# Two turns reordered: the last stage's step 0 begun in chunk 13, and the expert sums moved behind the scan

## The chip, the cores and the metric

The kernel runs on one core of a Trainium2 chip. The metric is the device time of one execution in microseconds (us), the median of a few runs. TensorE (PE) multiplies into eight PSUM banks, VectorE (DVE), ScalarE (ACT) and GpSimd (POOL) work elementwise, SyncE (SP) issues most DMAs; each runs its own queue of instructions in order and waits on semaphores for the others.

## The reference

A block on x of shape (8, 256, 32, 32): a layer norm over channels, a selective scan over 1024 tokens in a permuted order, a residual, then a mixture of experts on tokens.

```python
xz = silu(einsum('oc,bchw->bohw', in_proj_w, ln_c(x)) + in_proj_b)      # 256 -> 768
x_ssm, res, gate = split(xz, 3, axis=1)
xf = silu(conv1d_depthwise(x_ssm, dw_w, 3 taps) + dw_b)
dbc = einsum('oc,bcn->bon', dbc_w, xf) + dbc_b                          # dt, B, C per head
# two heads; x, softplus(dt), B, C gathered by perm (argsort of a Moebius score)
h = exp(dt * A) * h + dt * B * x;  y = sum_s(h * C) + D * x             # S = 8, 1024 steps
x = x + silu(out_proj(gather(y, inv) * silu(gate) + res) + out_b)
t = tokens(x);  u = ln_t(t)
w = softmax(u @ gate_w + gate_b); w = w * (w >= 0.1); w = w / sum(w)
out = t + sum_e w[:, e] * (u @ expert_w[e] + expert_b[e])               # 8 experts, 256 -> 256
```

## The kernel before

Float32 is multiplied as a high and a low part in fp32r (split3: three products). There are three stages, written out engine by engine, with an order set by hand.

Stage 1 takes the eight images ("batches", b = 0 to 7): norm, input projection (in_proj, L1211, weights win), convolution, and for each token a row of x, dt, B and C, stored to HBM (store_rows, L450) and later gathered by rank (gather_rows, L713). The residual and gate parts go to HBM from rg (L492, L501). Batch 7 is woven with the begin of stage 2. In it TensorE also runs expert_sums (L1298 to L1306), sums over the channels of the expert and gate weights, which are needed only in stage 3, and VectorE copies them in bias_rows. Batch 6's rows are stored by ScalarE here (L949).

Stage 2 is the scan, in 16 chunks q of 64 tokens for two heads of four images. For each: sums of dt (sums_of), B and C turned to rows (rows_of, L1268) and split to high and low (ScalarE rows_high L927, VectorE rows_low L1907) in the tile r6, which SP stores to bc_scratch (L457) and loads back spread over partitions (spread: eight loads L464 into cr, one L466 into bl); sums of dt between pairs of tokens (times_of, L1277) and from these dists (L1897); columns (L1317), which waits for r6 of the chunk after; eight products of B and C (products, L1332) in three banks, which VectorE multiplies by ScalarE's exponentials (decays L1012, times_decay L1947 and L1950); GpSimd adds six of these (add_state, L750); VectorE joins the sum to the tile kbd (whole_kernel, L1962); the chunk after runs y (y_states L1383, y_kernel L1391), which ScalarE copies out (y_rows L1026) and SP stores. cr and rg, the latter as ee, take over memory of stage 1, so parts of cr are set to zero behind the last in_proj (zero_rows L1816, and ScalarE L1047 for half of cr1). GpSimd issues the gathers of the rows three chunks ahead, and in chunks 9 to 12 (gather_first, L761) those of y for the first half image of stage 3.

Stage 3 takes 16 half images v (two for an image). For each: y gathered into token order and transposed (L1446), times gate (first_gate L2186, gate_y L2023), plus residual on GpSimd (first_z L773, z_of L825), high and low (z_high L1067, low_z L2029), out_proj (L1473) into banks FRONT_BANKS = (5, 4) for step 0, silu (L1077), residual x (L2046), transposes to tokens (L1485), statistics (L2053) and rstd on GpSimd (L829), gate logits (L1495, L1504), softmax (softmax_in, gate_exp L1097, softmax_out), whose weights TensorE transposes (weights_by_experts), and 16 products of experts (L1531). One step's front is woven into the experts of the step before; step 0's front is woven into chunks 14 and 15 (first_y_by_channels, first_gate and first_z in body(q), the rest in last_body and last_chunks). The z of all steps is split into zh and zl, in the first half columns of xhl, which is also cr[0].

## Time and profile before

| | us |
|---|---|
| median of 3 runs | 957.85 (956.61 to 958.96) |
| profiled execution | 963.8 |
| its span, first to last instruction | 962.1 |
| PE busy | 881.6 (92%) |
| DVE busy | 738.8 (77%) |
| ACT busy | 515.9 (54%) |
| POOL busy | 483.9 (50%) |

Times in the rows are us from the start of the span. Stage 1 ends near 244, stage 2 runs to about 461 and overlaps with stage 3's step 0. Busy shares are means over stages of unlike kind, so the page alone doesn't tell what bounds a turn. A row in order of time gives start, duration, line, tiles, and in brackets the idle time of the engine before it, with what ended it.

### The profile page before, as it was taken

What the parts mean: (1) busy time and instruction counts of PE and PEld (TensorE: products, weight loads), DVE (VectorE), ACT (ScalarE), POOL (GpSimd) and SP (SyncE); (2) the same over time, 40 slices, a digit from 0 to 9 for tenths busy, and PEclk for the clock granted to TensorE, in tenths of its full rate; (3) what the DMA queues carried; (4) which work ended last, traced back from release to release, by engine and by line L of the source; (5) the groups of instructions that cost most, each with busy time, mean ns of one, the idle gap of its engine ahead of it and who ended that gap; (6) DMA issues with size and microseconds to landing.
All of it is one profiled execution on the core that took longest, in us unless ns stands there. A gap on an engine that the chain in (4) does not pass through costs nothing.

```text
span 962.1 us, 15548 instructions
## 1 busy us (share of the span) xinstructions
PE 881.6 (92%) x4568; PEld 684.7 (71%) x4568; DVE 738.8 (77%) x2010; ACT 515.9 (54%) x1011; POOL 483.9 (50%) x552
## 2 busy tenths in 40 slices
PE   5999999899588788777999999999999999999997
PEld 4888888787355455545777777778777877777776
DVE  5769888564588888876878788787878877878875
ACT  4788777765799999885332333333233323323320
POOL 2165578885678787878363424244144442341100
PEclk8999999999688988979999999999999999999999
DMA  6235775466445544543530402304114132040000
GB/s 179 104 119 179 203 204 183 140 132 166 126 118 163 175 143 149 176 118 121 202 100 23 175 30 77 133 22 157 40 44 153 38 131 71 22 174 22 22 20 25
DMA packets 63689, 110.07 MB, mean 114 GB/s; under 512 B 18538, under 2 KB 44436, under 8 KB 60564
## 3 DMA queue, kind: packets, MB, share of 16 engines
q1 hardware_dynamic: 54388, 90.23, 29.6%
q0 software_dynamic: 7168, 18.03, 6.6%
q10 hardware_dynamic: 2080, 1.19, 0.8%
q8 instruction: 23, 0.38, 0.2%
q14 instruction: 30, 0.25, 0.1%
HBM read 61.51 MB, written 47.92 MB: 114 GB/s over the span
## 4 chain that ended last, share of the span: by engine, by line
PE 61%; DVE 13%; POOL 9%; DMA 6%; ACT 5%; issue 5%; SPq 1%; another core or an unknown queue 0%; DVEq 0%; POOLq 0%; ACTq 0%
PE bank L1531 33%; POOL sm L750 6%; PE bank L1211 6%; PE bank L1473 5%; PE bank L1446 3%; PE bank L1495 2%; DVE ssm L2023 2%; PE bank L1332 2%; PE bank L1391 2%; DMA score_scratch<-score 1%; PE bank L1383 1%; PE bank L1222 1%; PE bank L1485 1%; ACT dtri L1020 1%; PE bank L1520 1%
## 5 line engine op out<-in xcount | busy, mean ns | idle before, releaser
L813 POOL DMA_INDIRECT xtm<-y_scratch,idxu x112 | 116.2, 1037 | 75.7 <-DVE idxu L2015 44.8
L1531 PE MATMUL bank<-wexph,xhl 128*128 128x512 f32 x512 | 143.3, 401 | 1.3 <-DVE xhl L2068 1.3
L1531 PE MATMUL bank<-wexph,cr 128*128 128x512 f32 x512 | 142.4, 400 | 0.0
L825 POOL TENSOR_TENSOR ssm<-ssm,rg 128x512 f32<-128x512 f32 x30 | 35.2, 1195 | 149.1 <-DVE ssm L2023 149.1
L1531 PEld LDWEIGHTS bank<-wexph,xhl 128*128 128x128 f32 x512 | 93.3, 188 | 22.7 <-issue 2.1
L1531 PEld LDWEIGHTS bank<-wexph,cr 128*128 128x128 f32 x512 | 93.5, 188 | 20.2
L750 POOL TENSOR_TENSOR sm<-sm,rg 128x512 f32<-128x512 f32 x80 | 102.7, 1284 | 6.1
L1012 ACT ACTIVATE rg<-dists,aown 128x512 f32<-128x512 f32 x128 | 82.0, 723 | 5.7 <-POOL sm L750 5.7
L1947 DVE TENSOR_TENSOR rg<-rg,bank 128x512 f32<-128x512 f32 x112 | 72.3, 680 | 15.6 <-PE bank L1332 13.8
L1531 PE MATMUL bank<-wexpl,xhl 128*128 128x512 f32 x256 | 80.7, 396 | 0.0
L1531 PE MATMUL bank<-wexpl,cr 128*128 128x512 f32 x256 | 80.4, 395 | 0.0
L1072 ACT ACTIVATE ssm<-bank,outb 128x512 f32<-128x512 f32 x30 | 20.6, 688 | 85.3 <-PE bank L1473 52.8
L2139 DVE SCALAR_TENSOR_TENSOR xf<-bank,soft,xf 128x256 f32<-128x256 f32 x128 | 57.1, 478 | 10.0 <-remote 8.4
L2139 DVE SCALAR_TENSOR_TENSOR ysb<-bank,soft,ysb 128x256 f32<-128x256 f32 x128 | 57.1, 478 | 7.3 <-PE bank L1531 5.2
L877 ACT ACTIVATE rg<-bank,inb 128x512 f32<-128x512 f32 x64 | 43.4, 687 | 35.2 <-PE bank L1211 33.6
L1211 PE MATMUL bank<-xhl,winh 128*128 128x512 f32 x192 | 57.2, 421 | 3.9 <-ACT ssm L877 2.9
L1147 ACT ACTIVATE stage<-bank 128x512 f32<-128x512 f32 x32 | 17.5, 596 | 73.9 <-PE bank L1446 70.5
L1211 PE MATMUL bank<-cr,winh 128*128 128x512 f32 x192 | 55.6, 412 | 1.3 <-ACT rg L877 0.6
L1531 PEld LDWEIGHTS bank<-wexpl,xhl 128*128 128x128 f32 x256 | 48.3, 189 | 11.6
L1531 PEld LDWEIGHTS bank<-wexpl,cr 128*128 128x128 f32 x256 | 48.2, 188 | 11.3
L829 POOL TENSOR_TENSOR rstd<-mv,root 128x4 f32<-128x4 f32 x16 | 16.6, 1041 | 77.3 <-DVE mv L2059 77.2
L2144 DVE SCALAR_TENSOR_TENSOR ysb<-bank,soft,ysb 128x256 f32<-128x256 f32 x128 | 55.5, 475 | 0.0
(329 smaller groups left out, 2077.7 us busy)
## 6 DMA issues: line engine op xcount, KB each, us to landing
xin<-in_x SPq DMA_DIRECT2D x16, 1024.0 KB, 6.9
res_gate_scratch<-rg SPq DMA_DIRECT2D x16, 1024.0 KB
rg<-res_gate_scratch SPq DMA_DIRECT2D x8, 2048.0 KB
y_scratch<-ysb SPq DMA_DIRECT2D x16, 512.0 KB, 2.9
out<-stage SPq DMA_DIRECT2D x16, 512.0 KB, 2.7
rows_scratch<-stage SPq DMA_DIRECT2D x8, 580.0 KB
bc_scratch<-r SPq DMA_DIRECT2D x16, 288.0 KB
rows_scratch<-xr SPq DMA_DIRECT2D x6, 580.0 KB
```

The source lines that it names most:

```text
L750: pool.tensor_tensor(ksum[c.two], ee[:, 0, :] if s == 1 else ksum[c.two], ee[:, s, :], ALU.add).then_inc(summed.sem, 1)
L813: pool.indirect_dma_start(out=xtm[:, t, h * P:(h + 1) * P], out_offset=None, in_=y_d[b // GB].rearrange("q p s c -> (q p s) c"), in_offset ...
L825: pool.tensor_tensor(z[:, k, :], z[:, k, :], rg[:, k, cols], ALU.add).then_inc(z_ready.sem, 1)
L877: act.activation(dst, bank[2 + hf][:, :], ACT.Silu, bias=inb[:, m:m + 1]).then_inc(mm_used[hf].sem, 1)
L1012: act.activation(ee[:, s, :], dist[c.two].rearrange("p t n -> p (t n)"), ACT.Exp, scale=aown[:, s:s + 1]).then_inc(e_ready.sem, 1)
L1211: last = pe.matmul(bank[2 + hf][:, :], w[:, k, m * P:(m + 1) * P], v[:, k, cols], start=(n + k == 0), stop=(n + k == 3))
L1446: last = pe.transpose(dst[:, i * P:(i + 1) * P], src(i), ident[:, :])
L1473: last = pe.matmul(bank[banks[m]][:, :], w[:, k, m * P:(m + 1) * P], x_[:, k, :], start=(n + k == 0), stop=(n + k == 3))
L1531: last = pe.matmul(bank[4 + i][:, :], x_[:, k, i * P:(i + 1) * P], w[:, 2 * ep * KC + k:2 * ep * KC + k + KC + 1:KC, :], start=(n + k == 0 ...
L1947: dve.tensor_tensor(ee[:, s, :], ee[:, s, :], bank[BC_BANK + s % 3][:, :], ALU.mult).then_inc(bc_used[s % 3].sem, 1)
L2139: dve.scalar_tensor_tensor(ttm[par][:, i, :], bank[4 + i][:, 0:C], soft[par][:, 1, i, 2 * ep:2 * ep + 1], ttm[par][:, i, :], ALU.mult, ALU ...
L2144: dve.scalar_tensor_tensor(ttm[par][:, i, :], bank[4 + i][:, C:2 * C], soft[par][:, 1, i, 2 * ep + 1:2 * ep + 2], ttm[par][:, i, :], ALU.m ...
```

## The change

It has two parts. At the first turn: expert_sums leaves batch 7 and is cut in three parts (12, 10 and 10 matmuls, now into bank 0), set between TensorE's work after chunk 15's products; bias_rows follows statistics3; batch 6's rows are stored by SP, at the head of its batch 7, instead of by ScalarE; chunk 1's rows_of, rows_high and rows_low come before chunk 0's first product; the upper part of cr1 is set to zero by GpSimd in one memset of 128x3072 behind the gathers of chunks 2 and 3, instead of by VectorE (128x1024) and ScalarE (128x2048).

At the second turn: first_y_by_channels, first_gate and first_z move from chunk 14 to chunk 13; z_high and low_z follow in chunk 14, and zh and zl lie now in win's tiles; out_proj's halves come before chunk 15's products 1 and 4; on GpSimd three gathers leave the midst of chunk 15's additions and stand behind them with the two that were there; ScalarE takes chunk 15's columns, and an exponential of one column, earlier. All work of the kernel before is still done. The diff, cut to one line of context:

```diff
@@ -201,7 +201,8 @@
 gate_sums = sb("gate_sums", [P, E])
-ones = hs[1][:, :]
+cw1 = sb("all_ones", [P, P])
+ones = cw1[:, :]
...
@@ -225,7 +226,7 @@
        for v in (xf[:, 0, :], ysb[0][:, :, :].rearrange("p s n -> p (s n)"))]
-zh, zl = (xhl[:, v, :, 0:HALF] for v in range(2))
+zh, zl = (w[:, :, :].rearrange("p k c -> p (k c)")[:, 0:KC * HALF].rearrange("p (k n) -> p k n", n=HALF) for w in win)
...
@@ -457,7 +458,7 @@
 if c.q == 1:
-    sync.wait_ge(cr_zero[1], 5)
+    sync.wait_ge(cr_zero[1], 4)
...
@@ -487,6 +488,8 @@
     load_experts(b)
+if b == NB - 1:
+    store_rows(b - 1)
...
@@ -732,10 +735,14 @@
 up_to_token(Chunk(1))
-softplus_ratio(softplus_power(NB - 1))
...
 gather_rows(Chunk(3))
+last_front = softplus_power(NB - 1)
+for hf in range(2):
+    pool.wait_ge(mm_full[hf].sem, mm_full[hf].at(NB, 0))
+pool.memset(cr1[:, 2:S, :].bitcast(F32), 0.0).then_inc(cr_zero[1], 1)
+softplus_ratio(last_front)
...
@@ -775,10 +782,8 @@
 for s in range(1, S - 1):
-    if q == CHUNKS - 2 and s in (S - 3, S - 2):
+    if q == CHUNKS - 3 and s in (S - 3, S - 2):
         first_z(s - S + 3)
-    if q == CHUNKS - 1 and s == 3:
-        gather_first(1, second_half[3:6])
...
@@ -800,7 +805,7 @@
 if q == CHUNKS - 1:
-    gather_first(1, second_half[6:8])
+    gather_first(1, second_half[3:8])
...
@@ -912,13 +917,13 @@
     act.wait_ge(h_ready.sem, h_ready.at(c.q - 1, 0))
-if c.q == 0:
-    act.wait_ge(rows_split.sem, rows_split.at(0, 1))
+if c.q < 2:
+    act.wait_ge(rows_split.sem, rows_split.at(c.q, 1))
...
-if c.q:
+if c.q > 1:
...
@@ -940,14 +945,6 @@
                 act.activation(cwt[c.four][:, :], bank[A_BANK][:, 0:P], ACT.Copy).then_inc(cols_copied.sem, 1)
-
-            def store_rows(b):
-
-                act.wait_ge(rows_ready.sem, rows_ready.at(b, 4))
-                act.wait_ge(rows_staged.sem, rows_staged.at(b, 4))
-                for hf, v in enumerate(staged[b % 2]):
-                    act.dma_start(rows_d[b // GB][:, hf * TPH * HEADS:(hf + 1) * TPH * HEADS, b % GB, :],
-                                  v.rearrange("p t (h c) -> p (t h) c", h=HEADS)).then_inc(rows_stored[b % 2].sem, 16)
...
@@ -976,7 +973,6 @@
 block_decays(Chunk(0))
-store_rows(b - 1)
...
@@ -1038,14 +1034,11 @@
 c = Chunk(q)
-rows_high(Chunk(q + 1))
+if q:
+    rows_high(Chunk(q + 1))
+else:
+    state_decay(Chunk(1))
 block_decays(Chunk(q + 1))
-if q == 0:
-    act.wait_ge(kbd_zero, 1)
-    for hf in range(2):
-        act.wait_ge(mm_full[hf].sem, mm_full[hf].at(NB, 0))
-    act.activation(cr[1][:, S // 2:S, :], bc(kbd[:, 0:GB, :].rearrange("p t n -> p (t n)"), 1, S // 2),
-                   ACT.Copy).then_inc(cr_zero[1], 1)
...
@@ -1096,6 +1089,7 @@
+rows_high(Chunk(1))
...
@@ -1106,24 +1100,25 @@
 columns(c)
+z_high(0)
...
     y_rows(Chunk(CHUNKS - 3), h)
-z_high(0)
+columns(last)
 decays(last, 2, S)
-columns(last)
 first_silu_t(0)
-states_by_tile(last)
...
 x3_high(0, 0)
+states_by_tile(last)
...
 y_rows(c, 1)
+act.activation(std[:, 0:1], root[:, 0:1], ACT.Exp)
...
 y_rows(last, 0)
+gate_exp(0, 0)
 y_rows(last, 1)
-gate_exp(0, 0)
...
@@ -1274,6 +1269,8 @@
 pe.wait_ge(dist_set.sem, dist_set.at(c.q, 0))
+if c.q == CHUNKS - 1:
+    pe.wait_ge(y_gated.sem, y_gated.at(0, KC))
...
@@ -1291,20 +1288,21 @@
-            def expert_sums():
-
-                pe.wait_ge(kbd_zero, 6)
-                pe.wait_ge(wexp_low, WEXP_PARTS)
-                pe.matmul(bank[1][0:2 * E, 0:C], ident[0:E, 0:2 * E], expb[:, :], start=True, stop=False)
-                for e in range(E):
+            def expert_sums(lo, hi):
+
+                pairs = [(e, k, w) for e in range(E) for k in range(KC) for w in wexp]
+                if lo == 0:
+                    pe.wait_ge(kbd_zero, 6)
+                    pe.wait_ge(wexp_low, WEXP_PARTS)
+                    pe.wait_ge(h_ready.sem, h_ready.at(CHUNKS, 0))
+                    pe.matmul(bank[0][0:2 * E, 0:C], ident[0:E, 0:2 * E], expb[:, :], start=True, stop=False)
+                for e, k, w in pairs[lo:hi]:
+                    last = pe.matmul(bank[0][0:2 * E, 0:C], minus_one[:, E - 1 - e:3 * E - 1 - e], w[:, e * KC + k, :],
+                                     start=False, stop=(e, k) == (E - 1, KC - 1) and w is wexp[1])
+                if hi == len(pairs):
                     for k in range(KC):
-                        for w in wexp:
-                            last = (e, k) == (E - 1, KC - 1) and w is wexp[1]
-                            pe.matmul(bank[1][0:2 * E, 0:C], minus_one[:, E - 1 - e:3 * E - 1 - e], w[:, e * KC + k, :],
-                                      start=False, stop=last)
-                for k in range(KC):
-                    last = pe.matmul(bank[1][:, C:C + E], ones, gateraw[:, k, :], start=(k == 0), stop=(k == KC - 1))
-                last.then_inc(sums_full, 1)
+                        last = pe.matmul(bank[0][:, C:C + E], ones, gateraw[:, k, :], start=(k == 0), stop=(k == KC - 1))
+                    last.then_inc(sums_full, 1)
...
@@ -1323,7 +1321,6 @@
 pe.wait_ge(dskip_ready, 4)
-pe.wait_ge(sums_taken, 4)
...
@@ -1354,7 +1351,6 @@
 sums_of(Chunk(0))
-expert_sums()
...
@@ -1362,8 +1358,8 @@
 sums_of(Chunk(1))
+rows_of(Chunk(1))
 products(Chunk(0), 0, 1)
-rows_of(Chunk(1))
...
@@ -1406,14 +1402,14 @@
 products(c, 1, 4)
-if q == CHUNKS - 2:
+if q == CHUNKS - 3:
...
 products(c, 4, 6)
-if q == CHUNKS - 2:
+if q == CHUNKS - 3:
...
@@ -1431,15 +1427,16 @@
 columns(c)
+out_proj(0, FRONT_BANKS, 0, 1)
+products(c, 1, 4)
+out_proj(0, FRONT_BANKS, 1, 2)
+products(c, 4, 6)
...
     y_states(prior, h)
-products(c, 1, 4)
-out_proj(0, FRONT_BANKS, 0, 1)
-products(c, 4, 6)
-out_proj(0, FRONT_BANKS, 1, 2)
...
     y_kernel(prior, h)
+expert_sums(0, 12)
...
@@ -1449,7 +1446,7 @@
 pe.wait_ge(gathered[0].sem, gathered[0].at(1, 0))
-pe.wait_ge(dist_set.sem, dist_set.at(CHUNKS, 0))
+pe.wait_ge(dist_set.sem, dist_set.at(CHUNKS - 1, 0))
...
@@ -1465,7 +1462,8 @@
 if banks == FRONT_BANKS:
-    pe.wait_ge(cols_copied.sem, cols_copied.at(CHUNKS, 0))
+    pe.wait_ge(*((dist_set.sem, dist_set.at(CHUNKS, 0)) if lo == 0 else
+                 (cols_copied.sem, cols_copied.at(CHUNKS, 0))))
...
@@ -1575,12 +1573,14 @@
 y_states(Chunk(CHUNKS - 1), 0)
+expert_sums(12, 22)
...
 y_states(Chunk(CHUNKS - 1), 1)
+expert_sums(22, 2 * E * KC)
...
@@ -1813,7 +1813,8 @@
     dve.wait_ge(mm_full[hf].sem, mm_full[hf].at(b, 0))
-dve.memset(cr[i][:, 2:S if i == 0 else S // 2, :].bitcast(F32), 0.0).then_inc(cr_zero[i], 1)
+if i == 0:
+    dve.memset(cr[i][:, 2:S, :].bitcast(F32), 0.0).then_inc(cr_zero[i], 1)
...
@@ -1849,7 +1850,6 @@
 exponents(Chunk(0))
-bias_rows()
...
@@ -1965,13 +1965,11 @@
 c = Chunk(q)
-if q + 1 < CHUNKS:
+if 0 < q < CHUNKS - 1:
...
     whole_kernel(Chunk(q - 1))
-if q == CHUNKS - 1:
-    low_z(0)
...
@@ -1980,22 +1978,26 @@
 times_decay(c, 4)
-if q == CHUNKS - 2:
+if q == CHUNKS - 3:
...
 times_decay(c, 5)
-if q == CHUNKS - 2:
+if q == CHUNKS - 3:
...
 if q == CHUNKS - 1:
-    first_residual()
+    first_residual(0)
+    clear_wide(0, Chunk(q - 1))
+    first_residual(1)
...
     next_states(Chunk(q + 1))
+if q == CHUNKS - 2:
+    low_z(0)
...
@@ -2038,13 +2040,17 @@
-            def first_residual():
+            def first_residual(k):
...
                 dve.wait_ge(x3_ready.sem, x3_ready.at(0, 16))
-                for k in range(KC):
-                    dve.wait_ge(m3_free[k].sem, m3_free[k].at(0, 1))
-                    dve.tensor_tensor(tcm[:, k, :], bank[FRONT_BANKS[k]][:, :], xin[:, k, 0:HALF], ALU.add).then_inc(
-                        t_ready.sem, 1)
+                dve.wait_ge(m3_free[k].sem, m3_free[k].at(0, 1))
+                dve.tensor_tensor(tcm[:, k, :], bank[FRONT_BANKS[k]][:, :], xin[:, k, 0:HALF], ALU.add).then_inc(
+                    t_ready.sem, 1)
+
+            def clear_wide(par, c):
+
+                dve.wait_ge(k_ready.sem, k_ready.at(c.q, 2))
+                own.did(dve.memset(wide[par], 0.0))
...
@@ -2207,6 +2213,7 @@
 zero_rows(1, NB)
+rows_low(second)
...
@@ -2220,13 +2227,12 @@
 statistics3(front, 0, 0)
+bias_rows()
 shifts(front, 0)
-dve.wait_ge(k_ready.sem, k_ready.at(CHUNKS, 0))
-for v in wide:
-    own.did(dve.memset(v, 0.0))
-own.settle()
...
 front.end()
+clear_wide(1, Chunk(CHUNKS - 1))
+own.settle()
...
     step3(b, 1, True, b + 1)
```

## Rows read from the trace of the kernel before

**Rows 1.** Stretches: us, busy per engine (count), PEclk, DMA share, GB/s.

```profile
303.00:413.00 110.00, 87.99 (x505) 57.34 (x504) 91.12 (x216) 102.53 (x298) 91.35 (x79) 0.91 0.54 160
...
440.00:466.00 26.00, 21.15 (x102) 15.57 (x103) 18.30 (x47) 13.93 (x28) 16.51 (x15) 0.93 0.46 169
466.00:962.00 496.00, 482.39 (x2336) 380.58 (x2334) 392.48 (x1101) 151.02 (x228) 166.95 (x157) 1.00 0.22 76
```

**Rows 2.** Chain that ended last, chunks 0 to 3: start, us, what.

```profile
219.79 3.85 PE bank L1303 x32
...
238.03 5.80 DMA bl<-bc_scratch
...
243.88 0.80 PE bank L1332
...
322.39 3.06 DMA bl<-bc_scratch
```

**Rows 3.** SP's DMA issues: start, us, line, what.

```profile
207.05 1.00 SPq L450 DMA_DIRECT2D rows_scratch<-stage  x2
208.78 0.71 SPq L501 DMA_DIRECT2D res_gate_scratch<-rg  x1
...
230.82 0.50 SPq L457 DMA_DIRECT2D bc_scratch<-r  x1
234.17 3.82 SPq L464 DMA_DIRECT2D xhl<-bc_scratch  x8
...
268.30 2.72 SPq L464 DMA_DIRECT2D xhl<-bc_scratch  x8
```

**Rows 4.** DMA queue q1, 207 to 215.5: packets, MB, share.

```profile
q1 hardware_dynamic: 2080, 1.19, 96.1%
```

**Rows 5.** DMA queue q1, 228 to 231.9.

```profile
q1 hardware_dynamic: 144, 1.05, 63.8%
```

**Rows 6.** DMA queue q0 (gathers), 245 to 251.

```profile
q0 software_dynamic: 320, 1.19, 70.6%
```

**Rows 7.** POOL in order of time, batch 7 and chunk 0.

```profile
223.60 0.56 POOL L657 TENSOR_TENSOR xr<-dbx,xr 128x64 f32<-128x64 f32 x2
...
243.38 1.10 POOL L713 DMA_INDIRECT xr<-rows_scratch,turn  x1 [0.95 <-DMA rows_scratch<-xr]
...
253.18 1.29 POOL L750 TENSOR_TENSOR sm<-rg 128x512 f32<-128x512 f32 x1 [4.66 <-DVE rg L1947]
```

**Rows 8.** PE in order of time, chunk 0.

```profile
249.06 0.48 PE L1317 MATMUL bank<-ident,cw 128*128 128x128 f32 x1 [2.71 <-DVE r L1909]
```

**Rows 9.** POOL in order of time, chunks 12 to 15.

```profile
416.41 0.95 POOL L761 DMA_INDIRECT ssm<-y_scratch,idxu  x1 [0.30 <-issue]
...
429.28 1.28 POOL L750 TENSOR_TENSOR sm<-rg 128x512 f32<-128x512 f32 x1 [3.85 <-DVE rg L1947]
...
455.45 0.96 POOL L761 DMA_INDIRECT xtm<-y_scratch,idxu  x1
...
458.99 1.05 POOL L829 TENSOR_TENSOR rstd<-mv,root 128x4 f32<-128x4 f32 x1 [1.33 <-DVE mv L2059]
```

**Rows 10.** DMA queue q0 (gathers), 419 to 419.5.

```profile
q0 software_dynamic: 4, 0.00, 2.3%
```

**Rows 11.** PE in order of time, chunks 13 to 15.

```profile
415.44 1.91 PE L1383 MATMUL bank<-xf,cwt 128*128 128x512 f32 x2
...
419.59 1.02 PE L1383 MATMUL bank<-xf,cwt 128*128 128x512 f32 x2
...
433.36 0.66 PE L1446 MATMUL bank<-ident,ssm 128*128 128x128 f32 x4 [1.22 <-DVE ssm L2186]
...
465.52 0.61 PE L1446 MATMUL bank<-ident,sm 128*96 128x128 f32 x4 [0.64 <-DVE sm L2112]
```

**Rows 12.** DVE in order of time, chunk 14.

```profile
439.40 1.40 DVE L1962 TENSOR_TENSOR kbd<-sm,bank 64x512 f32<-64x512 f32 x2 [0.82 <-POOL sm L750]
```

**Rows 13.** ACT in order of time, end of chunk 15.

```profile
461.38 1.28 ACT L1097 ACT_TABLE_LOAD   x1
```

More of the change, by code:

```diff
@@ L1669, in bias_rows @@
                 for j in (0, 2):
-                    dve.tensor_copy(expb3[j * PART:j * PART + 2 * E, :], bank[1][0:2 * E, 0:C]).then_inc(sums_taken, 1)
-                dve.tensor_copy(gate_sums[:, :], bank[1][:, C:C + E]).then_inc(sums_taken, 1)
+                    dve.tensor_copy(expb3[j * PART:j * PART + 2 * E, :], bank[0][0:2 * E, 0:C]).then_inc(sums_taken, 1)
+                dve.tensor_copy(gate_sums[:, :], bank[0][:, C:C + E]).then_inc(sums_taken, 1)
                 dve.wait_ge(sums_taken, 3)
-                dve.tensor_tensor(expb3[PART:PART + 2 * E, :], bank[1][0:2 * E, 0:C], expb3[0:2 * E, :].bitcast(F32),
+                dve.tensor_tensor(expb3[PART:PART + 2 * E, :], bank[0][0:2 * E, 0:C], expb3[0:2 * E, :].bitcast(F32),
                                   ALU.subtract).then_inc(sums_taken, 1)
@@ L2024, in gate_y, with low_z @@
                                       ALU.mult).then_inc(y_gated.sem, 1)
-            def low_z(v):
-                for k in range(KC):
+            def low_z(v, lo=0, hi=KC):
+                for k in range(lo, hi):
                     dve.wait_ge(zh_ready.sem, zh_ready.at(v, k + 1))
@@ L2039, in residual @@
                                       ALU.add).then_inc(t_ready.sem, 1)
-            def first_residual():
+            def first_residual(k):
                 dve.wait_ge(x3_ready.sem, x3_ready.at(0, 16))
-                for k in range(KC):
-                    dve.wait_ge(m3_free[k].sem, m3_free[k].at(0, 1))
-                    dve.tensor_tensor(tcm[:, k, :], bank[FRONT_BANKS[k]][:, :], xin[:, k, 0:HALF], ALU.add).then_inc(
-                        t_ready.sem, 1)
+                dve.wait_ge(m3_free[k].sem, m3_free[k].at(0, 1))
[4 more added lines that the diff above has]
+                own.did(dve.memset(wide[par], 0.0))
             def statistics3(own, v, par):
```

## The prediction

> **What bounds the kernel now.** I read the windows by stage first, to see where an engine is full. The last stage, from 466 us, is TensorE's: 482.4 us busy of 496 at full clock [rows 1]. The change leaves it alone, so it can only be begun earlier or later. The scan's steady chunks, 303 to 413, are paced by GpSimd's additions and ScalarE (91.4 and 102.5 us busy of 110) [rows 1], and no chunk from 2 to 12 is edited. What is left are two turns: out of the input projection into chunk 0, and chunks 13 to 15 into the last stage. For these I read the chain of work, then the timeline of each engine, then the DMA queues in short windows.
>
> In the first turn the chain runs over the sums of the expert weights on TensorE (32 matmuls, 3.85 us), but it ends on a DMA: the last load of chunk 0's rows of B lands 5.80 us after its issue, and the first product starts at 243.88 [rows 2]. Work that ends earlier ahead of that load gains nothing by itself. In the second turn GpSimd's queue of gathers and additions leads to chunk 15's last addition at 455.3 (its next gather follows at 455.45), and TensorE begins the transposes of the expert weights at 465.52, after 0.64 us of waiting [rows 9, 11].
>
> **First turn: ahead of the first product.** The sums leave TensorE here: 3.85 us of matmuls and about 0.9 for bias and gate, 4.7 in all, and VectorE's copies behind them. Batch 7 ends some 5 us earlier, so the store of r6 (bc_scratch) that SP issued at 230.82 could be issued near 225.5. What is late next is the queue. The store of batch 6's rows moves from ScalarE's queue to SP's, and is issued when GpSimd has finished these rows, 223.60 + 0.56 = 224.2 [rows 7], which the change doesn't hasten. On SP's queue stand then, in order: rows store, residual store, r6 store. The same pair of rows store and a 1 MB store was issued by SP at 207.05 and 208.78 [rows 3]; from 207 to 215.5 the queue moved 2080 packets and 1.19 MB, which are the two row stores to the packet, and nothing of the 1 MB store behind [rows 4]. So one queue works in order, and a rows store holds it 8.4 us from its issue: 224.2 + 8.4 = 232.6. The residual store's 1.05 MB took at most 3.9 us [rows 5]; I take 2.8, so 235.4. The r6 store took 3.35 us from issue to its successor (230.82 to 234.17) [rows 3], of which I count 2.1 behind a full queue: 237.5. Nine loads are issued in 2.7 + 0.3 us when it is quiet (268.30) [rows 3], and the last lands 3.06 later in a quiet stretch [rows 2]: 243.6. Beside this lie the gathers of chunks 2 and 3, which wait for the same rows store (243.38 before, now near 233) [rows 7] and keep 70.6% of the DMA engines for 6 us [rows 6]; they cost between nothing and 2.4, and I take 1.0, since only the r6 store lies in their midst. The first product: 244.6, against 243.88: **+0.7** (bounds -0.9 to +2.4).
>
> A rule of the Trainium skill speaks on this move, and for it: "DMA: Bandwidth & Descriptors", section Issuing engines are not separate DMA queues, says that DMAs run on the same 16 engines whoever issues them, and interleave, so that a choice of issuer is worth sequencer time alone. Read so, the move would cost nothing, and the first product would come some 5 us earlier. The packets between 207 and 215.5 don't bear this reading out within one queue; what it would give is the first rival.
>
> **After the first product.** Chunk 1's rows_of, rows_high and rows_low now stand before it, covered by the wait for the load. TensorE's columns waited 2.71 us for VectorE's rows_low [rows 8], and GpSimd's first addition came at 253.18, 9.3 us after the first product [rows 7]. With the wait gone, distances, second product and first addition follow earlier: **-2.7** (bounds -2.0 to -3.4, the upper with the 0.65 us of rows_of counted too). SP's spread for chunk 1 is issued earlier still and is covered. ScalarE's 1.9 us fill of cr1 becomes a GpSimd memset of 128x3072 floats. No such one is in the trace; by its 128x1024 ones, near 1 us, it costs 3, and it stands between two softplus steps that must be done by about 251, some 3 us later than I place them. I take nothing, and up to 1. ScalarE's own gain is not added: it waits for the first row transposes, which move by the same 2.7. First turn in sum: **-2.0** (-4.3 to +1.4). Chunks 2 to 12 carry it on, each being paced by its own work.
>
> **Second turn: chunk 13.** TensorE now transposes y of the last stage's step 0 after products 1 to 3 of chunk 13, where it began y_states at 415.44 [rows 11]. It must wait for all eight gathers of the first half. Their order on GpSimd is not changed: the last is issued at 416.41, ends at 417.36 [rows 9], and its packets run into 419 to 419.5 [rows 10]. In chunk 14 this wait was long over; in chunk 13 TensorE stands from 415.4 to 419.6: **4.1 us**. Behind it in TensorE's queue are y of chunk 12, products 4 to 7, sums, rows and states of chunks 14 and 15; behind these wait ScalarE's copy of y, then dtri of chunk 15, then r6 of chunk 15, then VectorE's kernel tile of chunk 13, that is, everything that starts chunk 14. The transposes themselves add 0.9, and the second four 0.66 with a wait of 1.22 for the gate before them [rows 11], 2.8 in all. That chain was the bound here: GpSimd stood idle 3.85 us before chunk 14's first addition [rows 9]. So with 4.1 + 2.8 = 6.9 us GpSimd's first addition of chunk 14 goes from 429.28 to 436.2. The two z additions lie in the wait for product 4 and cost nothing there; without cover, 1.3 each.
>
> **Chunk 14** loses this work: six additions in a row, 6 x 1.34 = 8.0, end at 444.2. Before, they ended at 439.4, where VectorE's kernel tile of the chunk starts [rows 12]: **+4.8**.
>
> **Chunk 15** loses the three gathers from its midst: three gathers (3.6) and six additions (8.0; VectorE's low parts beside them may add 0.6) end at 455.8 to 456.4, I take 456.2, against 455.3: **+0.9**. So the gathers taken out pay back 3.9 of 4.8.
>
> **After chunk 15.** GpSimd then has five gathers where it had two: 5 x 0.95 + 4 x 0.30 = 6.0, to 462.3, and only then the 1.05 us power for rstd, which was done at 460.04 [rows 9]; now 463.4. From there to TensorE's transposes took 5.5 us (465.52) [rows 11]; the exponential's table load, 1.28 us at 461.38 [rows 13], goes under cover by the added one-column Exp, and so does the 0.35 of ScalarE's copy ahead of it. 463.4 + 3.9 = 467.3. TensorE's own queue comes out near the same. From 440 to 466 it was 21.15 us busy at a clock of 0.93 [rows 1]; the 4.7 us of sums are added, and about 2.4 of out_proj's first half now lie before chunk 15's second product, 0.5 after the expert weights' transposes begin. So 22.9 us without idle time, some 1.2 less at full clock, counted from when the kernel tile of chunk 14 is done, 444.2 + 1.4 [rows 12] = 445.6: 467.3 to 468.5. VectorE's bias copies (1.4 us, the memset of 0.8 moved away) stay under GpSimd's delay. I take **+2.4** for the second turn (bounds +1.4 to +4.0; the lower if the wait for the gathers is 1 us shorter).
>
> For the table load, "ScalarE: Activation LUTs", section What ACT_TABLE_LOAD costs, says that a switch costs about 2.66 us with its drain. By that the cover would be worth 1.4 us more than by the row, where the exponential follows the load's end at once. Since TensorE's queue comes to the same time, the sum would stay.
>
> **Sum.** -2.0 + 2.4 = +0.4 on the profiled execution's 963.8 us, whose span is 962.1; it is 5.95 us above the median of the three runs, 957.85. The difference is taken over unchanged: **958.3 us**. The bounds together give 955.0 to 962.0.
>
> **Rivals.** (A) The row store holds nobody back: packets interleave, or its 7 us shrink. Then r6 is stored by 231, the loads land like before beside small packets, 9.7 us later at most (234.17 to 243.88), and the first product comes 3.3 to 7 us earlier than before. 0.4 - 0.7 - 5 gives 952.6. For it: the queue is idle from 221 to 228 in the trace, so work is moved into a hole. Against it: rows 4. Chance 0.27. (B) The wait in chunk 13 is hidden: GpSimd and ScalarE have enough in hand, and chunk 14 begins 3 us later rather than 7. Then 958.3 - 3.9 = 954.4. Against it: the chain over TensorE and ScalarE was the bound there already. Chance 0.10. (C), the slower side: the 4 us that TensorE stands still leave it at its lower clock. The y matmuls take 1.91 us at 415.44 and 1.02 at 419.59 for the same shape [rows 11]; at the lower level the second half of chunk 13, about 4 us of matmuls at full clock, takes 2.5 more, and the last stretch, with its sums, 1.2 more: 958.3 + 3.7 = 962.0. It decides if the granted clock stays low for over 3 us after the stall ends. Chance 0.21. That the change doesn't do what it says is in the forecast itself: the step is begun a chunk earlier and finished no earlier.
>
> **Chances.** The forecast (0.42) is the likeliest; most of its range lies within 0.3%, which is 2.9 us and about what a measurement of this kernel can tell from no change. Faster by over 0.3%: A and half of B, and a sliver of the forecast, 0.33. Slower: most of C and the upper edge of the forecast, 0.24. Same: 0.43. The range for 8 in 10 reaches from A's middle to C's: 952.3 to 962.3.
>
> **What would show it.** In the profile after: the r6 store of chunk 0 issued near 225.5, but followed by its loads only near 237.5; first product near 244.6; the first addition 6.6 us behind it; TensorE waiting about 4 us for DMA in its first transposes, in chunk 13; five gathers of about 6 us between chunk 15's last addition and rstd; TensorE's wait for the expert weights gone or small. The prediction is wrong if the loads follow the r6 store within 5 us of 225.5, if TensorE doesn't wait in chunk 13, or if the last stage's steps change their length.

## The result, and the profile after

The changed kernel took 966.01 us (median; 962.49 to 967.63) where the kernel before took 958.0 beside it: 1.0078 times, 95% interval 1.0064 to 1.0093. The forecast was 958.3 in a range of 952.3 to 962.3, so it is slower, and outside the range. Its profiled execution took 966.35 us (span 964.6), close to its median.

The stretches answer to [rows 1] (us, busy per engine, PEclk, DMA share, GB/s); this is the changed kernel.

```profile
303.00:413.00 110.00, 88.05 (x505) 57.24 (x504) 91.47 (x217) 102.88 (x299) 91.31 (x79) 0.90 0.55 161
...
440.00:471.00 31.00, 27.86 (x143) 20.72 (x143) 23.66 (x54) 15.61 (x30) 19.73 (x17) 0.89 0.47 170
471.00:964.00 493.00, 481.63 (x2338) 380.85 (x2335) 391.01 (x1099) 150.94 (x228) 166.32 (x157) 1.00 0.22 77
```

The last stage and the steady chunks are as they were: 481.6 us of TensorE at full clock against 482.4, and nearly the same clock (0.90 against 0.91) and busy shares from 303 to 413. What grew is what lies between. From 440 to the last stage's steady part TensorE is busy 27.9 us, not 21.2, at 0.89 of its clock, not 0.93.

First turn, chain of the changed kernel (start, us, what), then SP's issues, in order of time, which answer to [rows 2, 3]:

```profile
226.98 9.86 DMA bc_scratch<-r
239.73 5.56 DMA bl<-bc_scratch
245.33 0.80 PE bank L1329
```

```profile
224.40 0.99 SPq L451 DMA_DIRECT2D rows_scratch<-xr  x2
225.48 1.31 SPq L495 DMA_DIRECT2D res_gate_scratch<-rg  x1
226.98 1.13 SPq L458 DMA_DIRECT2D bc_scratch<-r  x1
236.94 2.75 SPq L465 DMA_DIRECT2D xhl<-bc_scratch  x8
```

GpSimd in the same stretch, in order of time, against [rows 7]:

```profile
235.27 1.10 POOL L716 DMA_INDIRECT xr<-rows_scratch,turn  x1 [9.88 <-DMA rows_scratch<-xr]
...
243.50 2.66 POOL L744 MEMSET cr<- 128x3072 f32 x1
...
251.20 1.28 POOL L757 TENSOR_TENSOR sm<-rg 128x512 f32<-128x512 f32 x1 [1.26 <-DVE rg L1947]
```

The absolute times of the first turn are close to the prediction's. The store of r6 stands behind the rows store and the residual store and lands 9.86 us after its issue at 226.98 (forecast near 225.5), its loads are issued at 236.94 (forecast 237.5), the first product starts at 245.33 (244.6), the first addition comes 5.9 us later (6.6). Only GpSimd's gathers are further off, at 235.27 (near 233). And yet the turn costs time, as the second trace of the kernel before shows below.

Second turn, TensorE and GpSimd, against [rows 9, 11]; then the chain from chunk 14's out_proj on:

```profile
418.63 1.12 PE L1443 MATMUL bank<-ident,ssm 128*128 128x128 f32 x4 [3.72 <-DMA ssm<-y_scratch,idxu]
...
443.24 1.22 PE L1471 MATMUL bank<-winh,wouth 128*128 128x512 f32 x2 [3.14 <-DVE winl L2031]
...
445.96 1.48 PE L1329 MATMUL bank<-cr,bl 128*128 128x512 f32 x3
...
470.75 0.60 PE L1443 MATMUL bank<-ident,sm 128*96 128x128 f32 x4
```

```profile
434.27 1.28 POOL L757 TENSOR_TENSOR sm<-rg 128x512 f32<-128x512 f32 x1 [4.39 <-DVE rg L1947]
...
447.56 1.28 POOL L757 TENSOR_TENSOR sm<-rg 128x512 f32<-128x512 f32 x1 [1.05 <-DVE rg L1947]
```

```profile
441.44 1.76 DVE winl L2031
443.24 2.92 PE bank L1471 x6
...
447.44 2.33 PE bank L1471 x6
...
454.20 0.53 PE bank L1298 x2
454.73 1.51 PE bank L1300 x12
...
457.97 1.20 PE bank L1300 x10
...
461.42 1.20 PE bank L1300 x10
```

TensorE waits 3.72 us in chunk 13 for the gathers, near the 4.1 forecast. Then, from 443.24 (after VectorE's low_z, 1.76 us its second step) to the transposes of the expert weights at 470.75, the chain never leaves TensorE: the sums (1.51, 1.20 and 1.20 us with 0.53 ahead) lie wholly on it, and the first half of out_proj takes 2.92 us where the second takes 2.33.

The granted clock behind the wait in chunk 13 (stretches as in [rows 1]):

```profile
415.30:418.60 3.30, 0.00 (x0) 0.00 (x0) 1.44 (x6) 2.77 (x8) 3.21 (x3) 1.00 0.61 187
418.60:421.50 2.90, 2.87 (x8) 1.83 (x9) 0.00 (x0) 0.28 (x1) 1.46 (x2) 0.50 0.20 60
```

The stretch in which TensorE stands still reads 1.00, so a mean over a longer window hides what comes behind it.

**How the traces are compared.** Absolute times shift by some us from one execution to the next. I use six marks: GpSimd's rows of batch 6 done (R), first product (P), GpSimd's first additions of chunks 0, 1 and 12 (A0, A1, A12), and TensorE's transposes of the expert weights (T). Each is the start of one row of the kinds shown here (R is the end of the row of xr<-dbx,xr). Differences in us:

| kernel | R to P | P to A0 | P to A1 | A12 to T |
|---|---|---|---|---|
| before, first trace | 19.72 | 9.30 | 25.43 | 61.07 |
| b_again | 15.27 | 8.76 | 25.60 | 61.56 |
| changed, first trace | 20.96 | 5.87 | 22.55 | 67.49 |
| a_again | 20.39 | 5.70 | 21.53 | 67.83 |
| s_front | 19.91 | 5.32 | 21.16 | 67.46 |
| sp_behind | 6.95 | 22.22 | 33.46 | 67.73 |
| r_act | 10.64 | 14.03 | 25.28 | 66.52 |
| t2_only | 14.20 | 8.76 | 26.03 | 66.11 |
| t1_only | 14.45 | 14.30 | 25.54 | 60.62 |
| t1_pool | 14.02 | 5.59 | 21.42 | 61.62 |
| t1_s | 12.07 | 14.04 | 25.30 | 63.42 |
| r_g | 11.48 | 14.31 | 25.57 | 61.70 |
| r_g_pool | 10.92 | 5.58 | 21.42 | 61.41 |
| sg_mid | 14.47 | 14.28 | 25.52 | 60.49 |

Where kernels have the same edits ahead of a mark, their differences agree within about 1.5 us, which is what one trace can tell; only the first trace of before falls out, from R to P, by 4.5 to 5.5 us. Between A1 and A12 no edit lies but r_g's (in r_g, r_g_pool and sg_mid); there the two traces of before took 135.1 and 134.8 us, but those of the changed kernel 135.4 and 132.1.

### The profile page after: what moved, and what is told of

The parts are those of the page before. It is cut to its first block, busy times and chain, and to the rows that moved or that the text cites. A ratio compares the mean times of both kernels' runs of the same rounds, so it can differ in the third digit from the quotient of the medians.

```text
span 964.6 us, 15547 instructions
## 1 busy us (share of the span) xinstructions
PE 875.9 (91%) x4568; PEld 682.3 (71%) x4568; DVE 735.8 (76%) x2009; ACT 514.0 (53%) x1011; POOL 489.2 (51%) x553
## 4 chain that ended last, share of the span: by engine, by line
PE 60%; DVE 12%; POOL 9%; DMA 7%; ACT 6%; issue 5%; SPq 1%; DVEq 0%; ACTq 0%; POOLq 0%
PE bank L1529 33%; PE bank L1471 5%; PE bank L1443 3%; PE bank L1206 3%; PE bank L1493 2%; PE bank L1379 2%; POOL sm L757 2%; PE bank L1329 2%; PE bank L1387 2%; ACT dtri L1016 2%; DVE ssm L2025 2%; DMA bc_scratch<-r 2%; DMA score_scratch<-score 1%; PE bank L1483 1%; ACT rg L1008 1%
## 5 line engine op out<-in xcount | busy, mean ns | idle before, releaser
L1065 ACT ACTIVATE ssm<-bank,outb 128x512 f32<-128x512 f32 x30 | 20.7, 691 | 83.8 <-PE bank L1471 83.8
L2145 DVE SCALAR_TENSOR_TENSOR xf<-bank,soft,xf 128x256 f32<-128x256 f32 x128 | 56.5, 478 | 1.4
L1206 PE MATMUL bank<-xhl,winh 128*128 128x512 f32 x192 | 54.7, 406 | 1.7 <-ACT ssm L882 0.6
L2150 DVE SCALAR_TENSOR_TENSOR xf<-bank,soft,xf 128x256 f32<-128x256 f32 x128 | 55.5, 475 | 0.0
```

What stands on the lines that cost most here:

```text
L1206: last = pe.matmul(bank[2 + hf][:, :], w[:, k, m * P:(m + 1) * P], v[:, k, cols], start=(n + k == 0), stop=(n + k == 3))
L2145: dve.scalar_tensor_tensor(ttm[par][:, i, :], bank[4 + i][:, 0:C], soft[par][:, 1, i, 2 * ep:2 * ep + 1], ttm[par][:, i, :], ALU.mult, ALU ...
L2150: dve.scalar_tensor_tensor(ttm[par][:, i, :], bank[4 + i][:, C:2 * C], soft[par][:, 1, i, 2 * ep + 1:2 * ep + 2], ttm[par][:, i, :], ALU.m ...
```

## The experiments

A ratio is to the kernel before on the same chip: 955.9 us beside b_again, r_act, s_front and t2_only, 957.4 beside a_again, t1_only, t1_s and r_g, 955.6 beside the others.

**b_again.** No edit.

> The kernel before, for a second profiled execution. Theory D (its first profiled execution, 5.8 us above its median, lost its time ahead of the scan and in the last stage): the first product comes near 240.2 instead of 243.9, the expert weights' transposes near 461.8 instead of 465.5, the last stage takes some 494 us instead of 496.6, and the span is near 956.5. Rival (the extra time lies somewhere else, or in all stages alike): the first product comes at 243.9 within 1 us again, and the difference of two profiles can be read as it stands.

958.39 us, span 956.7, last stage 494.7. Its chain, and its transposes (TensorE in order of time):

```profile
215.60 3.85 PE bank L1303 x32
...
226.63 3.24 DMA bc_scratch<-r
...
240.00 0.80 PE bank L1332
```

```profile
461.98 0.61 PE L1446 MATMUL bank<-ident,sm 128*96 128x128 f32 x4 [0.64 <-DVE sm L2112]
```

Theory D holds. The sums begin at 215.60, not at 219.79 [rows 2], and the first product at 240.00. The trace that the prediction read had lost about 4 us on TensorE ahead of the first turn and 2 in the last stage. t2_only, whose front is that of before, has the first product 14.20 us after R, beside 15.27 here and 19.72 in the first trace.

**a_again.** No edit.

> The changed kernel itself, beside the kernel before on the chip of the other runs, as their yardstick: by the first measurement 1.0078 times the time before, 963.3 to 964.5 us where the kernel before takes 955.9.

964.57 us, 1.0074 (1.0056 to 1.0093).

**r_act.**

```diff
 # SyncE, batch 7
-                if b == NB - 1:
-                    store_rows(b - 1)
 # ScalarE, batch 7, behind block_decays(Chunk(0)); its store_rows is that of before, not shown
+                    store_rows(b - 1)
```

> The changed kernel with one thing undone: the store of batch 6's rows is issued by ScalarE again, not by SP ahead of the residual store and the store of r6. Theory Q (in SP's queue it held the store of r6 for 8 us, but GpSimd's work from its gathers at 235.3 on, 14.7 us without a pause, is the nearer bound for the first addition): the loads of r6 follow its store by some 3 us instead of 10, the first product comes at 238 to 241 instead of 245.3, the first addition gains at most 1.3 us, and the time is 964.5 to 966. Rival 1 (the queue was what cost the turn): 961. Rival 2 (the queue held nobody): first product at 245.3 as before.

956.39 us, 1.0003 (0.9988 to 1.0018). ScalarE's issue, SP's issues, the first product (TensorE in order of time), and the chain of waits from the rows store on:

```profile
223.69 1.47 ACTq L952 DMA_DIRECT2D rows_scratch<-xr  x2
```

```profile
221.17 0.50 SPq L458 DMA_DIRECT2D bc_scratch<-r  x1
225.16 4.26 SPq L465 DMA_DIRECT2D xhl<-bc_scratch  x8
229.46 0.31 SPq L467 DMA_DIRECT2D bl<-bc_scratch  x1
```

```profile
234.26 0.79 PE L1336 MATMUL bank<-xhl,bl 128*128 128x512 f32 x1 [2.46 <-DMA bl<-bc_scratch]
```

```profile
224.12 8.62 DMA rows_scratch<-xr
...
238.42 2.94 POOL sp L606
...
241.77 2.66 POOL cr L742
244.42 2.91 POOL sp L614
```

The rows store's place on SP, then, cost the turn: the same store runs for 8.62 us, but the loads of r6 are issued 11.0 us earlier, counted from R. Two things make up the 11.0. SP takes its instructions in order and stood waiting for GpSimd's rows before it could issue anything behind the rows store: r6's store is issued 2.4 us before R here and 2.6 after it in the changed kernel, 5.1 in all. The other 6.0 lie between that issue and the loads' (4.0 us here, 10.0 there), where the store of r6 stands behind the two others. The loads don't escape the rows store quite: from 226 to 230 SP's queue moved 69 packets and ScalarE's 1335, in the next 2 us 598 and 63. Rival 1 was nearest, and even it gave too little. Theory Q was right on the queue and wrong on its price, and it put the first product at 238 to 241, where it came at 234.26. Counted from R the first addition gains 2.2 us and chunk 1's 7.6 (35.92 against 43.51; 6.0 against a_again), since GpSimd's late start is made up inside chunk 0: A0 to A1 is 11.3 us here and 16.7 in the changed kernel. What the chain shows instead is GpSimd's own work behind the gathers (2.94, 2.66 and 2.91 us), the next bound.

**sp_behind.**

```diff
-                if b == NB - 1:
-                    store_rows(b - 1)
 ...
                     spread(Chunk(0))
+                    store_rows(b - 1)
```

> The changed kernel, the rows store still on SP's queue, but issued behind the spread of chunk 0 (store and loads of r6) instead of ahead of the residual store. Theory Q (a queue works in order; what is behind the rows store waits, what is ahead doesn't): the first product comes some 11 us after GpSimd's rows of batch 6 are done, instead of 20.4, though the same DMAs run. But the gathers of chunks 2 and 3 wait for the rows store, begin near 243, and 14.7 us of GpSimd's work stand behind them: first addition near 258, time 964 to 967, no better than the changed kernel. Rival 1 (SP's issuing or the shared DMA engines are what delays the loads): first product at 18 to 20 us still. Rival 2 (the first product, not GpSimd, sets the time): 957.

962.34 us, 1.0065 (1.0041 to 1.0089). SP's issues, the first product, GpSimd:

```profile
220.97 0.50 SPq L458 DMA_DIRECT2D bc_scratch<-r  x1
224.66 2.74 SPq L465 DMA_DIRECT2D xhl<-bc_scratch  x8
...
227.86 1.03 SPq L451 DMA_DIRECT2D rows_scratch<-xr  x2
```

```profile
230.35 0.50 PE L1328 MATMUL bank<-xhl,bl 128*128 128x512 f32 x1 [0.33 <-DMA bl<-bc_scratch]
```

```profile
237.81 1.10 POOL L715 DMA_INDIRECT xr<-rows_scratch,turn  x1 [13.39 <-DMA rows_scratch<-xr]
...
252.57 1.26 POOL L756 TENSOR_TENSOR sm<-rg 128x512 f32<-128x512 f32 x1
```

Same issuer, same DMAs, another order: the first product comes 6.95 us after R instead of 20.4. So it is the order of SP's work (what SP waits for first, and what stands first in its DMA queue) that costs 13 to 14 us, not the time SP takes for issuing. The DMA engines that both issuers share cost less, 3.7 us: that is what r_act, whose loads run against the rows store, takes longer from R to P. The time gains nothing measurable, as GpSimd's gathers now come late: the first addition is at 252.57, sooner than the 258 expected (I had the gathers 5 us too late).

**t1_only.** The first turn's reordering alone, on the kernel before: rows_of(Chunk(1)), rows_high and rows_low ahead of the first product, cr1's fill as in the change.

```diff
 # before.py, TensorE and ScalarE; VectorE's rows_low(second) likewise
+                    rows_of(Chunk(1))
                     products(Chunk(0), 0, 1)
-                    rows_of(Chunk(1))
 ...
+            rows_high(Chunk(1))
             decays(Chunk(0), 0, 2)
 ... # GpSimd
-            softplus_ratio(softplus_power(NB - 1))
 ...
             gather_rows(Chunk(3))
+            last_front = softplus_power(NB - 1)
 ...
+            pool.memset(cr1[:, 2:S, :].bitcast(F32), 0.0).then_inc(cr_zero[1], 1)
+            softplus_ratio(last_front)
```

> The kernel before with the first turn's reordering alone: rows of B and C and the transposes of chunk 1 ahead of the first product, the memset of cr1 on GpSimd. The rows store stays with ScalarE, the sums stay in batch 7, the second turn is as before. Theory O (the reordering gives what the prediction took for it, 2.7 us, and the other 3.4 of the 6.1 us by which r_act reached chunk 1's first addition earlier came from the sums that left the front): 953.2, first product within 0.5 us of where it was. Rival (all 6 us came from the reordering): 950. Rival 2 (it gives nothing): 956.

957.91 us, 1.0007 (0.9998 to 1.0015): rival 2. GpSimd, and ScalarE's decays of chunk 1:

```profile
254.79 1.26 POOL L754 TENSOR_TENSOR sm<-rg 128x512 f32<-128x512 f32 x1
```

```profile
256.14 1.33 ACT L1016 ACTIVATE rg<-dists,aown 128x512 f32<-128x512 f32 x2 [2.18 <-POOL sm L754]
```

The columns do come earlier (chunk 0's 1.8 us after the first product, 4.7 in b_again), but GpSimd, with the gathers moved ahead of its softplus steps and the memset among them, starts 14.3 us after the first product, and ScalarE waits for it.

**t1_pool.** t1_only, repaired:

```diff
+            softplus_ratio(softplus_power(NB - 1))
             pool.wait_ge(rows_stored[0].sem, rows_stored[0].at(NB // 2, 0))
             gather_rows(Chunk(2))
             gather_rows(Chunk(3))
 ... # with last_front and its waits
-            pool.memset(cr1[:, 2:S, :].bitcast(F32), 0.0).then_inc(cr_zero[1], 1)
-            softplus_ratio(last_front)
 # VectorE, zero_rows
-                if i == 0:
-                    dve.memset(cr[i][:, 2:S, :]...
+                dve.memset(cr[i][:, 2:S, :]...
```

> t1_only with GpSimd's queue ahead of the first addition as it was: the last softplus steps ahead of the gathers of chunks 2 and 3, and the memset of cr1 (128x3072) on VectorE. Theory G (in t1_only GpSimd, with gathers, 2.66 us of memset and 5.9 of softplus in a row, began its additions 14.3 us after the first product instead of 8.8, and ScalarE, 3 us earlier through the reordering, waited 2.18 us for it): the first addition comes 9 us after the first product, chunk 1's first addition 22.5 instead of 25.5 us after it, and the time is 2.5 to 3 us below t1_only, 954.7 to 955.5 where the kernel before takes 957.4. Rival (something else holds chunk 1, a load or VectorE's rows): no change, 957 to 958.

953.63 us, 0.9975 (0.9961 to 0.9988); t1_only stood at 1.0007. GpSimd:

```profile
244.75 1.29 POOL L750 TENSOR_TENSOR sm<-rg 128x512 f32<-128x512 f32 x1 [0.23 <-DVE rg L1945]
...
260.58 1.28 POOL L750 TENSOR_TENSOR sm<-rg 128x512 f32<-128x512 f32 x1 [6.62 <-DVE rg L1945]
```

Theory G holds, P to A1 falls from 25.54 to 21.42 us. So by the marks the reordering is worth 4.1 us by itself, and GpSimd's new order (softplus steps and memset together; they weren't taken apart) takes the 4.1 away unless the first product is so late that it is covered, as it was in the changed kernel. The times show less of it: 3.1 us between t1_only and t1_pool, 2.4 (1.1 to 3.7) against the kernel before.

**t2_only.** The second turn's edits on the kernel before, without the sums.

```diff
 # before.py, TensorE; first_gate, first_z, z_high, low_z, gathers as in the change
-                if q == CHUNKS - 2:
+                if q == CHUNKS - 3:
                     first_y_by_channels(0)
```

> The kernel before with the second turn's edits alone: the last stage's step 0 begun in chunk 13, out_proj and the gathers moved, the sums left in batch 7 and the first turn as it was. Theory T (the second turn is what makes the changed kernel slower: 4 us of waiting for the gathers in chunk 13, low_z and the first half of out_proj late, two fifths of the loss being the sums, which are absent here): 958.0 + 2.5 = 960.5. Rival (the loss stems from the first turn or from the sums alone): 958 to 958.5, same as before.

960.1 us, 1.0049 (1.0031 to 1.0067). Theory T holds, with 4.7 us instead of 2.5; A12 to T shows 4.6.

**s_front.**

```diff
 # TensorE, batch 7
                     sums_of(Chunk(0))
+                    expert_sums()
 # last stage, step 0 (and the parts 0-12 and 22-32 likewise)
-            expert_sums(12, 22)
```

> The changed kernel with the expert weights' sums and VectorE's copies of the bias rows put back into batch 7 of the input projection, all else as changed. Theory S (in the second turn TensorE works from chunk 14's out_proj to the transposes of the expert weights without a pause, so the sums' 4.7 us lie wholly on the path there, until GpSimd's rstd behind five gathers takes over, some 3.3 us sooner): tail 3.3 us shorter, front 0 to 1 us longer since the store of r6 waits behind the rows store anyway: 962.5 to 963.7. Rival (GpSimd's gathers are the bound and the sums are covered): gain under 1 us, 965 to 966.

962.59 us, 1.0071 (1.0047 to 1.0095), beside 1.0074. The times don't decide: theory S asked for 1.0047 to 1.006, which that interval holds. The marks do: A12 to T is 67.46 us, as in the changed kernel (67.49 and 67.83), where 3.3 less was expected. GpSimd, ScalarE and TensorE at the end of the turn:

```profile
457.48 1.07 POOL L834 TENSOR_TENSOR rstd<-mv,root 128x4 f32<-128x4 f32 x1
```

```profile
459.71 0.23 ACT L1090 ACTIVATE soft<-soft 128x32 f32<-128x32 f32 x1 [3.29 <-DVE soft L2090]
459.85 0.58 ACT L1022 ACTIVATE ysb<-bank 128x512 f32<-128x512 f32 x1
```

```profile
460.78 1.19 PE L1529 MATMUL bank<-wexph,xhl 128*128 128x512 f32 x4 [2.23 <-ACT ysb L1022]
...
462.59 1.91 PE L1529 MATMUL bank<-wexph,xhl 128*128 128x512 f32 x4
...
465.15 0.67 PE L1443 MATMUL bank<-ident,sm 128*96 128x128 f32 x4
```

Theory S falls. Without the sums TensorE runs ahead, and then waits 2.23 us for ScalarE's copy of y (0.58 us at 459.85). That copy stands behind the exponential, which waits for GpSimd's rstd (457.48), which stands behind five gathers. TensorE then works at its lower clock (granted 0.50 from 462.5 to 464.5: 1.91 us for four matmuls that take 1.19 in the row above). Both chains end at the same place, as the prediction had it, but each some 4 us later than it said.

**r_g.** r_act, and the gathers of the first half's y a chunk sooner:

```diff
-                if NT < q <= NT + TPH:
-                    gather_first(0, [(q - NT - 1, h) for h in range(HEADS)])
+                if NT < q < NT + TPH:
+                    gather_first(0, [(t, h) for t in range(TPH) for h in range(HEADS)][(0, 2, 5)[q - NT - 1]:(2, 5, 8)[q - NT - 1]])
```

> r_act (the changed kernel with the rows store given back to ScalarE) with one more edit: GpSimd's eight gathers of the first half's y stand behind the additions of chunks 9 to 11 (2, 3, 3) instead of 9 to 12 (2 each), so none is under way when TensorE transposes in chunk 13. Theory W (TensorE's wait for them, 4.9 us in r_act, pushes chunk 14 back one for one): the wait is gone, the first addition of chunk 14 comes 4 to 4.9 us earlier, time 952. Rival (ScalarE or GpSimd takes the place of the wait): at most 1.5 us, 955 or more.

954.87 us, 0.9977 (0.9962 to 0.9992); r_act stood at 1.0003. Chunks 9 to 11 now issue 2, 3 and 3 of the eight gathers. The first transposes in chunk 13, r_act, then r_g:

```profile
410.17 1.12 PE L1450 MATMUL bank<-ident,ssm 128*128 128x128 f32 x4 [4.94 <-DMA ssm<-y_scratch,idxu]
```

```profile
412.90 1.05 PE L1450 MATMUL bank<-ident,ssm 128*128 128x128 f32 x4
```

The wait of 4.94 us is gone and A12 to T falls by 4.8. But ahead of A12 the extra gathers lengthen chunks 10 and 11 on GpSimd from 12.9 to 14.2 us each (first addition to first addition), 2.5 in all. 4.8 - 2.5 = 2.3, and 2.5 were measured: theory W is right on the wait, and my expected 4 to 4.9 left out what its remedy costs.

**t1_s.** t1_only and the sums in the tail, nothing else of the second turn.

```diff
 # t1_only, TensorE; the sums' other parts and bias_rows likewise
-                    expert_sums()
 ...
+                expert_sums(0, 12)
```

> The reordering of the first turn and the sums moved to the tail, the rows store with ScalarE, the second turn's step 0, out_proj and gathers as before. Theory: the first turn gains 6.1 us as in r_act. In the tail TensorE stood idle some 5 us between 437 and 462 in the kernel before (1.13, 0.92, 2.00, 1.22 and 0.64 the largest waits), which takes up about half of the sums' 4.7 us: 952 to 953. Rival (the waits are for work that lies behind the sums on the same path, so the sums add in full): 954.5.

954.27 us, 0.9968 (0.9954 to 0.9983), A12 to T 63.42: the sums cost 1.9 to 2.8 there (61.56 in b_again, 60.62 in t1_only), and their leaving gives 2.4 to 3.8 in front (R to P 14.45 in t1_only, 12.07 here, 10.64 in r_act). Its profiled execution lies 8.3 us above its median, so I read only its turns, and they don't account for the time: against b_again they give 1.6 of the 3.1 us gained on the kernel before, against t1_only nothing of the 3.6. Where the rest comes from is open. By the times alone, beside r_g (954.87), it says that the second turn's rearrangement, even freed of its wait, is worth nothing that shows.

**sg_mid.** r_g with the sums in front (the edit of s_front) and three gathers back between chunk 15's additions.

```diff
+                    if q == CHUNKS - 1 and s == 3:
+                        gather_first(1, second_half[3:6])
                     add_state(c, s)
 ...
-                    gather_first(1, second_half[3:8])
+                    gather_first(1, second_half[6:8])
```

> r_g with the sums back in batch 7 and three of GpSimd's last five gathers back in the midst of chunk 15's additions. Theory C (at the end of the second turn two chains of nearly the same length end together, TensorE's queue with the sums, and GpSimd's gathers, rstd and the exponential; taking one away shows nothing, s_front, taking both shows it): from chunk 12's first addition to the transposes of the expert weights 57.5 to 59 us instead of 61.7 in r_g, which pays for what the sums cost in front (3.3): 954 to 956. Rival (a third chain binds): 61 to 62 us there, 958.

956.77 us, 1.0012 (0.9999 to 1.0026). Theory C is at best half right: A12 to T is 60.49, 1.2 below r_g where 2.7 to 4.2 were expected. A third chain ends close behind the two; which one, these runs leave open.

**r_g_pool.** r_g with the repair of t1_pool, whose diff it shares.

> r_g with the same repair of GpSimd's queue. If theory G holds, the gain adds to those of r_act and r_g: chunk 1's first addition 22.5 us after the first product instead of 25.6, 951.5 to 952.5 where the kernel before takes 957.4. Rival: 954.9 as r_g.

950.08 us, 0.9932 (0.9911 to 0.9953), faster than both kernels. P to A1 is 21.42, from 25.57 in r_g, and the two gains add: 2.5 us from the wait, 4.3 from GpSimd's queue.

## Why the prediction was wrong

8 us were lost; the prediction had 0.4.

**The difference taken over unchanged: the step that failed first (4.2 us).** The first turn was to give -2.0. It gave +2.2: +6.0 up to the first product (R to P 20.7, the mean of the two changed traces, against 14.7, the mean of b_again and t2_only, whose front is that of before) and -3.8 behind it (P to A1 22.0 against 25.8). The absolute time of the first product was right to 0.7 us. But the kernel before had its first product at 243.88 only because TensorE was 4 us late in that one execution, and there the turn hangs on TensorE (the sums, then r6). In the changed kernel it hangs on GpSimd's rows and a store, and a late TensorE is covered. A difference between two chains was read off an execution in which one of them was stretched. The 5.95 us between the profiled time and the median stood in the prediction, and "unchanged" was the wrong thing to do with it. Up to the first product the change cost 6.0, not 0.7: the rows store's place cost 10 (20.7 against 10.64 in r_act), and what else was changed there gave 4 back. By its own absolute times, from R (224.2) to the first product (244.6), the forecast had 20.4; set against 14.7 that is +5.7, and with -2.7 behind it +3.0, near what came. So the mechanism of this turn was right, and what it was compared with wasn't; the 0.7 us from the absolute time is no credit to the difference.

**After the first product**: sized at -2.7, measured -3.8 at chunk 1 (-4.1 in t1_pool against t1_only). Mechanism right. GpSimd's memset, taken at 3 us and covered, took 2.66 and was covered, but in this kernel only.

**Chunk 13**: wait forecast 4.1, measured 3.72 (5.04 in a_again, 4.8 to 5.0 in the four other traces with it). The first addition of chunk 14 forecast 6.9 later; 6.2 later than in the first trace of before, 8.2 between a_again and b_again. Right, and rival B (wait hidden) is out.

**Chunks 14 and 15**: the last addition forecast +0.9, measured +1.8 against the first trace (A12 to its end 52.69 against 50.85). Chunk 14 gives back 1.7 of the 2.1 us it was to, chunk 15 2.6 of its 3.9: before its first addition GpSimd waits 1.05 us for VectorE's product (447.56), which waits for TensorE's, and those now stand behind out_proj's first half (443.24). The prediction put that move at nothing for GpSimd.

**After chunk 15 (the other failed step; with chunk 15, 4 us)**: TensorE's queue was to start at 445.6 and take 21.7 to 22.9 us. Counted from A12 it started 1.5 us later: in this trace low_z took 3.28 us for its two steps beside GpSimd's additions, and the first half of out_proj ran at the lower clock behind a wait of 3.14 us. And it took 24.8 (445.96 to 470.75), at a granted clock of 0.93, the very one that I had counted with; so the lower clock isn't what I missed there. At full clock the 24.8 are 23.1, against 21.7. The forecast took off 2.4 us for the first half of out_proj, its time at the lower clock (2.41 us, granted clock 0.63 from 442.7 to 445.2 in the first trace); in b_again, at full clock, it took 1.40. That is 1.0 of the 1.4, and 0.4 stay open. From the last addition to the transposes it was to grow by 1.5 us; it grew by 4.6 (14.80 against 10.22). In all the second turn cost 6.4 (A12 to T 67.49 against 61.07), not 2.4.

The total is firm, its division isn't. The three other traces with this turn whole have A12 to T at 66.5 to 67.8, but in r_act low_z took 1.21 us and the total was 66.52. Over the four with the sums in it (the changed kernel's two, sp_behind, r_act) against the two of before, the last addition comes 2.7 us later (53.8 against 51.1) and the rest takes 3.4 more (13.6 against 10.2), so both terms were too small, +0.9 and +1.5. s_front shows that GpSimd's gathers would have held the same place without the sums, and r_g that the wait in chunk 13, taken out, gives 2.5 us of the time back.

2.2 + 6.4 = 8.6 by the marks, 8.0 by the times. The prediction's own bounds, -2.9 and +5.4, make 955.0 to 963.2, not the 962.0 that it gives; 966.01 lies outside of both.

**Rivals.** (A), the largest: the rows store does hold the store of r6 back, by 10 us from R to P (20.7 against 10.64 in r_act), so it is out. "DMA: Bandwidth & Descriptors" of the Trainium skill, section Issuing engines are not separate DMA queues, would have it that the issuer matters for sequencer time alone. r_act agrees that two issuers' DMAs share the engines, if unevenly (69 packets beside 1335). It and sp_behind disagree with the conclusion: r6's store didn't overtake what one issuer had queued before it (9.86 us to landing against 3.24), and putting the rows store back was worth nearly 7 us (1.0074 to 1.0003). Of the 11.0 us by which r6's loads moved, though, 5.1 were SP's wait for GpSimd's rows. (C) named the lower clock after the wait, and its sign came about: when the wait ends TensorE works at a granted clock of 0.50, its lower level of 1.2 GHz, in the 2.9 us shown (418.60 to 421.50), and again behind the 3.14 us that it stood before out_proj (0.53 from 443.2 to 449.8). But the kernel before has this too: 0.50 from 413 to 419, and 0.83 from 440 to 450. Over the last stretch the means are 0.89 and 0.93; by them TensorE's busy time holds 3.1 us and 1.5 us that full clock would have saved (an estimate: 27.9 x 0.11, 21.2 x 0.07). So of C's 3.7 us the 1.2 of the last stretch came about, and the 2.5 of chunk 13 didn't.

The two misses have the same sign, and the range was built from bounds around a sum whose base was off, so it couldn't hold them.

## What to carry to other kernels

If the profiled execution isn't at the median, find where it lost its time before taking differences, above all if the change moves the bound from one engine to another: a delay of the old chain's engine is then counted as a gain of the change. A store moved to another queue is priced by what is queued behind it there and by what the new issuer must wait for before it can issue it, and the small store on which the next stage hangs goes ahead of the large one, unless somebody waits sooner for that (in sp_behind GpSimd's gathers did). When an edit clears one chain, list what the other engines have between the same two points; here GpSimd's order had to be put right before the reordering paid.
